# Row maxima of a causal attention: turned by VectorE in SBUF and brought to the query operand over DRAM, instead of turned by TensorE in PSUM

## What is computed

```python
Q, K = rope(x_n @ Wq), rope(x_n @ Wk)        # 4 sequences, 16 heads, 2048 positions, 16 wide
scores = Q @ K.T / sqrt(16), masked causally
attn = softmax(scores); out = attn @ V        # softmax subtracts the largest score of each query
x = x + out @ Wo
x = x + relu(layernorm(x) @ w1 + b1) @ w2 + b2
```

## Time and profile before

| | |
|---|---|
| time, median of 3 runs | 2169.41 us (2165.36 to 2172.35) |
| the profiled execution | 2172.91 us, span 2171.2 us |
| busy: PE, DVE, ACT, POOL | 2008.1, 1902.2, 1457.4, 637.1 us |
| mean granted clock of TensorE | 0.967 |
| L714 transposes / L812 / L819 | 64 each: 17.6 / 13.6 / 17.3 us busy |

### The profile page before, as it was taken

The page is one execution under the profiler, slowest core; times in us unless marked ns, Lnnn a source line. Parts: engine busy times, 40 slices in busy tenths (PEclk is TensorE's granted clock), DMA queues, the critical chain, the costliest instruction groups (busy, mean ns, idle before and its releaser), DMA issues. The chain is left out here.

```text
span 2171.2 us, 53576 instructions
## 1 busy us (share of the span) xinstructions
PE 2008.1 (92%) x19136; PEld 790.4 (36%) x19136; DVE 1902.2 (88%) x3974; ACT 1457.4 (67%) x3092; POOL 637.1 (29%) x1265
## 2 busy tenths in 40 slices
PE   5786599999999999999999999999999969999999
PEld 3444122222222222222222222222222237766776
DVE  8998899999999999999999999999999337777775
ACT  5664078888888788888888788888887742333222
POOL 7999421120221202221121211212212123332231
PEclk9999599999999999999999999999999889999999
DMA  5567331230313303033130322303120212222220
GB/s 193 203 220 209 122 70 37 51 65 17 72 27 64 61 22 66 21 76 50 33 66 17 76 35 52 66 17 74 27 52 13 69 39 78 82 94 84 87 78 29
DMA packets 126407, 152.64 MB, mean 70 GB/s; under 512 B 17248, under 2 KB 92512, under 8 KB 125920
## 3 DMA queue, kind: packets, MB, share of 16 engines
q1 hardware_dynamic: 126176, 149.67, 26.0%
HBM read 90.12 MB, written 59.24 MB: 69 GB/s over the span
## 5 line engine op out<-in xcount | busy, mean ns | idle before, releaser
L868 ACT ACTIVATE s_prob<-s_ps 128x512 f32<-128x512 f32 (+3 forms) x2560 | 1179.3, 540 | 276.5 <-PE s_ps L723 267.3
L797 DVE TENSOR_REDUCE s_part<-s_ps 128x2 f32<-128x1024 f32 x768 | 909.1, 1222 | 42.7 <-PE s_ps L706 25.1
L742 PE MATMUL s_ps<-s_prob,s_v 128*32 128x256 f32 (+3 forms) x10240 | 744.4, 363 | 8.4 <-POOL s_prob L898 0.9
L723 PE MATMUL s_ps<-aq,ak 64*128 64x512 f16 (+3 forms) x2560 | 674.5, 355 | 7.2 <-DVE s_part L804 1.2
L706 PE MATMUL s_ps<-mk,mq 64*128 64x512 f16 (+3 forms) x2560 | 590.7, 355 | 60.4 <-DVE s_part L797 28.1
L898 POOL TENSOR_SCALAR_AFFINE_SELECT s_prob<-s_prob 128x128 f32<-128x128 f32 x1024 | 286.7, 292 | 1170.7 <-ACT s_prob L868 1158.2
L804 DVE CUSTOM_DVE_ANT_0 s_ps<-s_ps,mask_sb 128x512 f32<-128x512 f32 (+3 forms) x1024 | 472.3, 520 | 25.9 <-PE s_ps L706 20.6
L723 PEld LDWEIGHTS s_ps<-aq,ak 64*128 64x128 f16 x2560 | 180.9, 93 | 524.0 <-ACT s_prob L868 439.9
L742 PEld LDWEIGHTS s_ps<-s_prob,s_v 128*32 128x32 f32 x10240 | 202.2, 108 | 464.4 <-issue 378.3
L706 PEld LDWEIGHTS s_ps<-mk,mq 64*128 64x128 f16 x2560 | 141.0, 95 | 105.4 <-DVE s_part L797 48.9
L1166 ACT ACTIVATE s_h_f<-s_ps,s_b_s 128x512 f32<-128x512 f32 x128 | 87.9, 687 | 105.9 <-PE s_ps L1031 85.0
(11 more groups left out here) (86 smaller groups left out, 1562.1 us busy)
## 6 DMA issues: line engine op xcount, KB each, us to landing
v_scratch<-s_vst SPq DMA_DIRECT2D x32, 512.0 KB, 3.9
s_v<-v_scratch SPq DMA_DIRECT2D x16, 1024.0 KB, 10.8
att_scratch<-s_o SPq DMA_DIRECT2D x64, 256.0 KB, 2.4
aq<-qk_scratch SPq DMA_DIRECT2D x96, 128.0 KB, 4.3
ak<-qk_scratch SPq DMA_DIRECT2D x96, 128.0 KB, 6.9
s_xin<-x SPq DMA_DIRECT2D x16, 512.0 KB, 4.4
qk_scratch<-s_r_lo SPq DMA_DIRECT2D x64, 128.0 KB, 2.2
qk_scratch<-s_r_hi SPq DMA_DIRECT2D x64, 128.0 KB, 2.4
```

Source lines behind the costliest of these rows:

```text
L723: nc.tensor.matmul(ps[:, s_bank(s, j), q0:CH], ak[rows, p, j // 2, kb * P:(kb + 1) * P], aq[rows, p, j // 2, c * CH + q0:(c + 1) * CH], st ...
L742: last = nc.tensor.matmul(ps[32 * j:32 * j + 32, O_BANK, cols], v[:, p, kb, j, :], prob[:, s % 2, j, cols], start=kb == 0 and part == 0, s ...
L797: nc.vector.tensor_reduce(part[:, qt // TPC, :, pair, qt % TPC, kc], ps[:, bank_of(use):bank_of(use) + 2, 0:w], AX.X, ALU.max).then_inc(m_ ...
L868: nc.scalar.activation(prob[:, s % 2, j, q0:CH], ps[:, s_bank(s, j), q0:CH], ACT.Exp, scale=1.0 / (SQK * DK ** 0.5)).then_inc(p_done, 1)
```

## The change

The maxima of a chunk are no longer turned by TensorE. `qmax` is 32 columns wide (16 used, the rest zero); VectorE transposes it in blocks of 32 x 32 from SBUF to SBUF (`turn_chunk`), scales it into `nrow`, now 128 partitions of 32 values, and SP writes that to a DRAM scratch with one DMA (`store_rows`) and reads it back into the two rows of `aq` with two (`load_rows`). The whole group on VectorE comes after both pairs of the step in which the last maxima are taken (`ended(t + 1)`), which is one step earlier than before. `max_rows` and its two uses of PSUM banks per chunk are gone. SP's list is written anew, and a wait on `pv_done` before `load_a` is left out. In the last iteration's masked steps 20-23 and 36-39, where no maxima are left, TensorE computes pairs of tiles that nothing reads (`filler_pair`); at step 20 it first waits until VectorE has read all maxima.

```diff
-        qmax = sb("s2_qmax", [P, NC, G * TPC], F32)
-        nrow = sb("s2_nrow", [G * TPC, NC, P], F16)
+        qmax = sb("s2_qmax", [P, NC, TURN], F32)
+        qmax_t = sb("s2_qmax_t", [P, NC, TURN], F32)
+        nrow = sb("s2_nrow", [P, NC, TURN], F16)
...
+        def ended(t):
+            return [(i, c) for i in (t // NS - 1, t // NS) for c in range(NC)
+                    if 0 <= i < NIT and t == NS * i + MAX_END[c]]
...
         def m_use(t, j):
-            return G * t + j + ROWS_TILES * rows_before[t]
+            return G * t + j
...
-            def rows(i, c):
-                sp.wait_ge(m_read, NM + rows_use(i, c) + ROWS_TILES)
-                for j in range(G):
-                    row = HROWS * (j % 2) + MAXROW
-                    k = TPC * (NP * (j % 2) + j // 2)
-                    sp.dma_start(aq[row:row + 1, i % 2, j // 2, c * CH:(c + 1) * CH], nrow[k:k + TPC, c, :]
+            def store_rows(i, c):
+                sp.wait_ge(nrow_done, NC * i + RANK[c] + 1)
+                sp.dma_start(rows_d[i, c].rearrange("r (u x) -> u r x", x=TURN), nrow[:, c, :]).then_inc(rows_out_done[c], 16)
+
+            def load_rows(i, c):
+                sp.wait_ge(rows_out_done[c], 16 * (i + 1))
+                for jj in range(2):
+                    row = HROWS * jj + MAXROW
+                    sp.dma_start(aq[row:row + 1, i % 2, :, c * CH:(c + 1) * CH],
+                                 rows_d[i, c, NP * TPC * jj:NP * TPC * (jj + 1), :].rearrange("(n q) x -> n (q x)", n=NP)
                                  ).then_inc(rows_in[c], 16)
...
-            def max_rows(i, c):
-                use = rows_use(i, c)
-                pe.wait_ge(qmax_done, NC * i + RANK[c] + 1)
-                pe.wait_ge(m_read, use + ROWS_TILES)
-                nc.tensor.transpose(ps[0:G * TPC, bank_of(use), 0:P], qmax[:, c, :], ident[:]
-                                    ).then_inc(m_ready, ROWS_TILES)
+            def filler_pair(p, s, pair):
+                qt, kc = MAX_TILES[(s + LAG) % NS]
+                for jj in range(2):
+                    rows = slice(HROWS * jj, HROWS * (jj + 1))
+                    nc.tensor.matmul(ps[:, M_BANK + 2 * pair + jj], mq[rows, p, pair, qt * P:(qt + 1) * P],
+                                     mk[rows, p, pair, 0:CH], start=True, stop=True)
...
+                    if t == STEPS_M:
+                        pe.wait_ge(m_read, NM + m_use(STEPS_M, 0))
...
                     if t < STEPS_M:
                         max_pair(t, 0)
+                    elif is_diagonal(s):
+                        filler_pair(p, s, 0)
...
+            def turn_chunk(i, c):
+                dve.wait_ge(qmax_done, NC * i + RANK[c] + 1)
+                nc.vector.transpose(qmax_t[:, c, :], qmax[:, c, :]).then_inc(turned, 1)
+
             def rows_out(i, c):
-                use = rows_use(i, c)
-                dve.wait_ge(m_ready, use + ROWS_TILES)
-                dve.wait_ge(rows_in[c], 16 * ROWS_DMAS * i)
-                nc.vector.tensor_scalar(nrow[:, c, :], ps[0:G * TPC, bank_of(use), 0:P], -1.0 / SQK, None, ALU.mult
+                dve.wait_ge(turned, NC * i + RANK[c] + 1)
+                dve.wait_ge(rows_out_done[c], 16 * i)
+                nc.vector.tensor_scalar(nrow[:, c, :], qmax_t[:, c, :], -1.0 / SQK, None, ALU.mult).then_inc(nrow_done, 1)
...
+                for i, c in ended(t + 1):
+                    max_of_chunk(i, c)
+                    turn_chunk(i, c)
+                    rows_out(i, c)
```

More of the change, by code:

```diff
@@ L58 @@
 LAG = NS // 2
+TURN = 32
 def is_diagonal(s):
@@ L530, in sem @@
             return ctx.enter_context(nc.semaphore(name))
-        ident, mask = ops.ident, ops.mask
+        mask = ops.mask
         mq, mk, aq, ak, m_in, a_in = ops.mq, ops.mk, ops.aq, ops.ak, ops.m_in, ops.a_in
@@ L549, in stage2 @@
         m_ready, m_read = sem("s2_m_ready"), sem("s2_m_read")
-        qmax_done = sem("s2_qmax_done")
+        qmax_preset, qmax_done, turned, nrow_done = sem("s2_qmax_preset"), sem("s2_qmax_done"), sem("s2_turned"), sem("s2_nrow_done")
         w_in, w_scaled, whi_done, w_done = sem("s2_w_in"), sem("s2_w_scaled"), sem("s2_whi_done"), sem("s2_w_done")
         masking, selecting = sem("s2_masking"), sem("s2_selecting")
+        rows_out_done = [sem(f"s2_rows_out{c}") for c in range(NC)]
         rows_in = [sem(f"s2_rows_in{c}") for c in range(NC)]
@@ L566, in stage2 @@
         STEPS_M = NIT * NS
-        def rows_after(t):
-            return [(t // NS, c) for c in range(NC) if t % NS == MAX_END[c]] if t % NS else \
-                [(t // NS - 1, c) for c in range(NC) if t > 0 and MAX_END[c] == NS]
-        rows_before = [0]
-        for t in range(STEPS_M + 1):
-            rows_before.append(rows_before[-1] + len(rows_after(t)))
+        RANK = [sum(e < MAX_END[c] for e in MAX_END) for c in range(NC)]
+        def ended(t):
+            return [(i, c) for i in (t // NS - 1, t // NS) for c in range(NC)
+                    if 0 <= i < NIT and t == NS * i + MAX_END[c]]
         def m_use(t, j):
-            return G * t + j + ROWS_TILES * rows_before[t]
-        def rows_use(i, c):
-            t = NS * i + MAX_END[c]
-            return G * min(t + 1, STEPS_M) + ROWS_TILES * (rows_before[t] + rows_after(t).index((i, c)))
+            return G * t + j
         def bank_of(use):
@@ L598, in read_before @@
             return ST * i + last_in_bank + 1
-        RANK = [sum(e < MAX_END[c] for e in MAX_END) for c in range(NC)]
         def crosses_diagonal(qt, kc):
@@ L639, in iteration @@
             def iteration(i, p, first=False, last=False, load2=True):
+                store_rows(i, 1)
                 if not first:
                     store(i - 1, NC - 1)
-                rows(i, 1)
+                load_rows(i, 1)
+                store_rows(i, 2)
+                store(i, 0)
+                load_rows(i, 2)
                 if not last:
-                    if not first:
-                        sp.wait_ge(pv_done, NS * i + 2)
                     load_a(sp, ops, qk_d, i + 1, 1 - p)
                     load_v(i + 1, 1 - p)
-                rows(i, 2)
                 if not first:
                     load_sums(i - 1)
-                store(i, 0)
                 store(i, 1)
@@ L655, in iteration @@
                     store_rinv(i - 1)
+                store_rows(i, 3)
+                load_rows(i, 3)
                 if load2:
@@ L659, in iteration @@
                     load_m(sp, ops, qk_d, i + 2, p)
-                rows(i, 3)
                 if last:
@@ L671, in iteration @@
                 if not last:
-                    rows(i + 1, 0)
+                    store_rows(i + 1, 0)
+                    load_rows(i + 1, 0)
             load_v(0, 0)
@@ L676, in _ @@
                 sp.dma_start(dst[:], src.rearrange("(k p) n -> p k n", p=P)).then_inc(w_in, 16)
-            rows(0, 0)
+            store_rows(0, 0)
+            load_rows(0, 0)
             iteration(0, 0, first=True)
@@ L771, in iteration @@
                         max_pair(t, 1)
+                    elif is_diagonal(s):
+                        filler_pair(p, s, 1)
                     value_step(i, p, s, 1)
-                    if t <= STEPS_M:
-                        for of, c in rows_after(t):
-                            max_rows(of, c)
             for t in range(LAG):
@@ L1225, in layer @@
     att_d = nc.dram_tensor("att_scratch", (NIT, P, S), F32, kind="Internal").ap()
+    rows_d = nc.dram_tensor("rows_scratch", (NIT, NC, TURN, P), F16, kind="Internal").ap()
     rinv_d = nc.dram_tensor("rinv_scratch", (NIT, G, S), F32, kind="Internal").ap()
```

23 lines of the change are left out of this document (8 added, 15 removed).

## The result

The changed kernel takes 2129.91 us (median of 4 runs, 2128.16 to 2130.91), the kernel before 2167.39 us (4 runs, 2165.07 to 2172.35). The ratio is 0.9824, with an interval of 0.9811 to 0.9836. The forecast of 2135 us lay 5 us above. The profiled execution took 2130.91 us, with a span of 2129.2 us: 42.0 us less than the span of before.

The account below looks back on a forecast made before the run. Mid-attention was taken as one coupled loop of TensorE and VectorE, neither dominating. 2172.9 - 28 (turning) - 6.4 (end of attention) + 0.3 (presets) = 2138.8, less 3.5 to the median: 2135 us, range 2116 to 2158.

Parts of the forecast that it names:

- The turning: Per iteration in attention: 3.28 us of turning cost removed, 1.5 us new cost, so 1.8 us gained, 28 us over 15.5 iterations.
- The group on VectorE: Reduction, transpose and scaling of one chunk, each waiting for the one before: 0.70 us of VectorE per chunk.
- Chunk 3, in front of its masked group: Step 19: VectorE runs through the masked group without a break, so 0.6 us reaches the loop.
- the three others: Chunks ending at steps 39, 3 and 23, where VectorE has idle time: 0.2 us each reaches the loop.
- Half a mask instruction of GpSimd, 0.3 us: Steps 0 and 20: VectorE's scaling collides with GpSimd's 0.29 us mask over shared ports; 0.3 us per iteration in all.
- The way over DRAM at nothing: SP's write, wait and two reads take 3.4 to 5.4 us, covered by other steps at every chunk, so cost nothing.
- The cover at step 4: Time left between chunk 1's rows landing and the step that needs them: 1.3 us.
- The end of attention, 6.4 us: After the maxima run out: unread matmuls keep TensorE's clock up, saving 8.0 us less 0.8 for them and 0.8 for waiting.
- The sum: Whole kernel: 2172.9 - 28 - 6.4 + 0.3 (two more presets ahead of the stage) = 2138.8, less 3.5 to the median.

## Why the prediction was right, and where its terms were off

**The turning.** Right in mechanism, and the sum was too small. What turning cost before was put at 3.28 us per iteration, against a floor of 3.08 by the kernel without it. The group on VectorE was put at 0.70 us and measures 0.71 (0.22, 0.21 and 0.18 us, and a start 0.03 us behind the end of the one before each time). The error is in how much reaches the loop: 1.5 us forecast, 0.93 measured. Chunk 3, in front of its masked group, costs 0.49 + 0.22 = 0.71 (0.6 forecast); the three others, 0.2 each in the sum, cost 0, 0 and 0.18. The loop gave 32.0 + 1.3 = 33.3 us instead of 28.

**Half a mask instruction of GpSimd, 0.3 us.** This term should not have been there. Timeline of DVE and POOL of the changed kernel at step 20:

```profile
1127.35 0.20 DVE L822 TENSOR_SCALAR s_nrow<-s_qmax_t 128x32 f16<-128x32 f32 x1
```

```profile
1127.22 0.29 POOL L899 TENSOR_SCALAR_AFFINE_SELECT s_prob<-s_prob 128x128 f32<-128x128 f32 x1 [20.10 <-ACT s_prob L869]
```

The scaling starts 0.13 us into the mask and takes 0.20 us. So it is at step 20 of all iterations but the last: 15 scalings overlap a mask and take 200 to 205 ns, the other 49 take 181 or 182. All 64 of them, minimum, median and maximum in ns:

```profile
L822 DVE TENSOR_SCALAR s_nrow<-s_qmax_t x64: 181/182/205, 236.8 to 1665.6; 128x32 f16<-128x32 f32 x64
```

The Trainium skill, page "SBUF — State Buffer", section "Who interferes with whom", has the later of the two wait for the whole other instruction; that would have been 0.16 us more, and it was 0.02. The row decides against the term. Whether the scaling runs in the two-port mode to which the page ties this wait, no row shows.

**The way over DRAM at nothing.** Right as the changed kernel has it, no step waits. The cover at step 4 was put at 1.3 us; the reads are issued by 1086.09 and one more trip makes step 4 wait some 0.75 us. That the order of SP's queue was what carried this term was not in the prediction, which costed the order at nothing in itself: with the old one, rows of chunk 2 come late, and the whole gain is lost.

**The end of attention, 6.4 us.** This step failed, though the number came close: "If the clock holds, 6.4 us net" took the fall of the earlier trace rows for something that the kernel does and the 32 unread pairs for its cure. The kernel without the pairs holds the clock, one run with them fell, and a second execution of the kernel before has no long fall. The sizes were near: the long fall costs 7.7 us (8.0 forecast), the unread pairs 1.1 and the wait for all maxima 0.9 (0.8 each); a fall of 3.4 us in the changed kernel, 1.2 us, was not in the sum. That gives 7.7 - 1.1 - 0.9 - 1.2 = 4.5 us. The comparison of the two profiled executions did show it (47.8 against 42.4 us, less the wait's 0.9), but against a run of before without that fall, the second trace, the span gained is 2164.5 - 2129.2 = 35.3 us. The medians differ by 37.5.

**A term that was missing.** TensorE's clock falls for 3.41 us at a time in mid-attention, two or three times in each of the four traces of kernels with TensorE's transposes, and never in the seven traces of kernels that turn on VectorE (or not at all) with their rows in time. Table of windows of before, 6 us around one of them:

```profile
1196.00:1202.00 6.00, 5.60 (x53) 1.57 (x51) 4.48 (x20) 3.36 (x9) 2.31 (x9) 0.72 0.37 102
```

Each costs 1.4 to 1.5 us by the lengths of the iterations, together 4.4 here. All eleven lie in steps 1 and 2, just behind step 0, in which chunk 1 is turned and which takes 2.56 us instead of 1.91. Why they go is argued and not isolated: TensorE's idle time around the turning is shorter now. It fits that falls come back in all three kernels whose rows are late (9, 3 and 30 in attention), and there mostly behind TensorE's waits.

**The sum.** 28 + 6.4 - 0.3 = 34.1 us were forecast between the profiled executions; measured are 33.3 (turning) + 4.4 (short falls) + 4.5 (end, 5.4 less the wait's 0.9) - 0.2 (0.5 ahead of attention, less 0.2 behind it) = 42.0. The forecast then took off 3.5 us more, because the execution lay above its median, although the fall that it had just counted as a gain was the likely cause of that. So part of the closeness is luck: turning was put 5 us too low and the short falls at nothing, and against this stood 6.4 us for a fall that most executions of the kernel before do not have.

## What to carry to other kernels

Price a moved group of small instructions by what its engine does next: ahead of a stretch without idle time it costs in full, ahead of idle time hardly anything, and spread between independent instructions it costs a fraction. A stretch at the lower clock in one execution's trace is a term of the sum only when a second execution shows it. When a transfer becomes a chain of two, look at what stands between its two parts in the queue. A late arrival costs its wait once, and here about as much again where TensorE's granted clock fell behind the wait; read the clock before blaming the loop.

## What was not expected of the hardware

- The same kernel had 20.5 us at 1.2 GHz in the last 20 steps of attention in one execution and none in another; 7.7 us of time hang on it.
- Behind waits of TensorE for late rows the granted clock fell to 0.50 for 3.4 to 10.2 us, in the kernel with two more trips nearly each time; two steps that take 4.76 us at 1.00 took 6.9 there.
- A DMA of 8 KB, alone 0.54 us in SP's queue, took 6.36 and 7.28 us there behind some 13 loads.
- A VectorE instruction that waits for its own engine's result started 0.03 us after the end of that one, where one without the wait started 0.09 us before it; three in a row took 0.71 us of VectorE, and 0.31 apart.
- A scaling on VectorE that ran beside a GpSimd mask in SBUF took 200 to 205 ns instead of 182.
